# Query projections of a first attention: their evacuation moved from VectorE to ScalarE

## The reference

```
x_proj = (x @ w_in.T + b_in).reshape(b, l, 16, -1)     # 16 heads, 16 columns each for q, k, v
q, k, v = jnp.split(x_proj, 3, axis=-1)
att = jnp.einsum('blhd,bmhd->blmh', q, k) * scale      # scale = 1/sqrt(16)
att = jax.nn.softmax(att, axis=2)
opt = jnp.einsum('blmh,blhd->blhd', att, v)            # each row's own v, weighted by the sum over m
x = layernorm(x + opt @ w_out.T + b_out)
```

## Time and profile before

| | us |
|---|---|
| median of 3 runs (lowest, highest) | 3705.18 (3704.74, 3706.42) |
| the profiled execution: its time | 3707.26 |
| the profiled execution: span from first to last instruction | 3705.5 |
| busy, TensorE / VectorE / ScalarE / GpSimd | 3433.0 / 3400.8 / 2812.5 / 1788.8 |
| query evacuations on VectorE: 32 of them, busy | 23.9 |
| key evacuations on ScalarE: 32 of them, busy | 21.7 |

### The profile page before, as it was taken

How to read it: one execution, slowest core, us unless ns; L and a number is a source line. 1 busy time by engine, 2 the same in 40 slices (tenths; PEclk the granted TensorE clock), 3 DMA queues, 4 the chain that set the end, 5 groups by cost and what they waited for, 6 DMA issues and landing times. The chain is left out here.

```text
span 3705.5 us, 45135 instructions
## 1 busy us (share of the span) xinstructions
PE 3433.0 (93%) x14464; PEld 1298.0 (35%) x14464; DVE 3400.8 (92%) x5376; ACT 2812.5 (76%) x3033; POOL 1788.8 (48%) x1251
## 2 busy tenths in 40 slices
PE   8989998889999999899999999899999999899998
PEld 3334433432232324343232324343232324343333
DVE  7999999999999999889999999989999999467776
ACT  5998898778888888688888888688888887333333
POOL 4344333304444446455444446455444446758775
PEclk9999999899999999899999999899999999999999
DMA  5222222200010001200010101200000000100000
GB/s 166 80 90 93 76 83 68 83 22 18 18 29 18 29 18 41 76 16 22 18 29 18 29 18 46 70 18 21 18 29 18 29 18 18 50 1 12 12 12 12
DMA packets 117215, 142.84 MB, mean 39 GB/s; under 512 B 33394, under 2 KB 100466, under 8 KB 116978
## 3 DMA queue, kind: packets, MB, share of 16 engines
q1 hardware_dynamic: 116978, 139.95, 12.4%
HBM read 89.55 MB, written 50.33 MB: 38 GB/s over the span
## 5 line engine op out<-in xcount | busy, mean ns | idle before, releaser
L1130 ACT ACTIVATE scores<-scores,nmax 128x2048 f32<-128x2048 f32 x1024 | 2042.0, 1995 | 315.5 <-DVE scores L1321 304.4
L985 PE MATMUL ps<-stack 96*128 96x512 bf16 x4792 | 1299.9, 388 | 122.0 <-DVE scores L1321 94.9
L894 POOL TENSOR_TENSOR facc<-facc,probs 128x1024 f32<-128x1024 f32 x443 | 1049.3, 2369 | 598.1 <-ACT probs L1240 530.2
L1321 DVE TENSOR_SCALAR_CACHE_REDUCE scores<-ps,lows 128x1024 f32<-128x1024 f32 x1024 | 1278.8, 1278 | 34.3 <-PE ps L985 28.2
L1321 DVE TENSOR_SCALAR_CACHE_REDUCE scores<-ps 128x1024 f32<-128x1024 f32 x1024 | 1216.9, 1217 | 25.6 <-PE ps L985 24.4
L985 PEld LDWEIGHTS ps<-stack 96*128 96x128 bf16 x4792 | 372.7, 99 | 1168.6 <-DVE scores L1321 658.9
L1380 DVE TENSOR_REDUCE smax<-ps 128x2 f32<-128x1024 f32 x512 | 621.0, 1220 | 123.0 <-PE ps L1050 121.9
L1050 PE MATMUL ps<-fk,fq 64*128 64x512 f32 x2048 | 564.2, 632 | 60.6 <-DVE smax L1380 46.1
L1065 PE MATMUL ps<-fq,fk 64*128 64x512 f32 x2048 | 546.2, 611 | 10.6 <-DVE smax L1380 4.8
L1085 PE MATMUL ps<-probs,vals 128*64 128x512 f32 x2048 | 532.3, 615 | 4.8 <-DVE oT L1428 4.8
L1240 ACT ACTIVATE probs<-ps 128x1024 f32<-128x1024 f32 x384 | 385.4, 1012 | 88.1 <-PE ps L1068 87.7
(11 more groups left out here) (129 smaller groups left out, 2175.9 us busy)
## 6 DMA issues: line engine op xcount, KB each, us to landing
stack<-qk_levels SPq DMA_DIRECT2D x768, 64.0 KB, 2.2
qk_levels<-fk SPq DMA_DIRECT2D x64, 384.0 KB, 2.4
probs<-in_L_attn_x SPq DMA_DIRECT2D x16, 512.0 KB, 4.1
v_rows<-vals SPq DMA_DIRECT2D x16, 512.0 KB, 2.9
vrows<-v_rows SPq DMA_DIRECT2D x16, 512.0 KB, 3.3
res<-in_L_attn_x SPq DMA_DIRECT2D x16, 512.0 KB, 4.0
x_rows<-y SPq DMA_DIRECT2D x16, 512.0 KB, 2.9
res<-x_rows SPq DMA_DIRECT2D x16, 512.0 KB, 3.9
```

Of the source, the lines that this page charges most:

```text
L894: pool.tensor_tensor(total, total, probs[:, slot, :], ALU.add).then_inc(facc_ready, 1)
L985: last = pe.matmul(bank(banks[i]), stack[0:SK, hd % 2, 0, t * P:(t + 1) * P], stack[0:SK, hd % 2, 1, col:col + CH], start=True, stop=True)
L1130: act.activation(row, row, ACT.Exp, bias=nmax[:, k % LOWS:k % LOWS + 1], scale=-1.0, accum_out=esum[:, b % 2, t, hd:hd + 1]).then_inc(exp_ ...
L1321: dve.tensor_scalar(scores[:, k % ROW_SLOTS, half * TILE:(half + 1) * TILE].rearrange("p (a n) -> p a n", a=2), two_banks(banks), 1.0, fir ...
```

## The change

Query halves are evacuated by ScalarE as `Identity(scale * in + bias)`, with the scale -1/4 in the instruction. Since the bias is now added after the scaling, the two bias columns of the queries are multiplied by -1/4 once at the start (one VectorE copy of four columns becomes a multiplication of two and a copy of two). In the planner the piece `QP` moves from VectorE to ScalarE, and the planned cost of a query or key evacuation goes from 0.75 to 0.6; so the planner works out all five lists anew.

```
-        for kind, eng in (("QP", dve), ("KP", act)):
+        for kind, eng in (("QP", act), ("KP", act)):
...
-            unit(eng(*t), 0.75, [pe(*t)] + ([was("LV", *two)] if i >= 2 else []))
+            unit(eng(*t), 0.6, [pe(*t)] + ([was("LV", *two)] if i >= 2 else []))
...
+                elif kind == "QP":
+                    i = half_no[at]
+                    act.wait_ge(wT_read, 4)
+                    if i >= 2:
+                        act.wait_ge(q_split, (i - 1) * LEVEL_STEPS)
+                    act.activation(q32[:, i % 2, :], bank(banks[0]), ACT.Identity, bias=qk_bias[:, at[1]:at[1] + 1],
+                                   scale=-float(AD) ** -0.5).then_inc(q32_ready, 1)
...
-            dve.tensor_copy(qk_bias[:, :], ps[:, 3, 0:4]).then_inc(wT_read, 1)
+            dve.tensor_scalar(qk_bias[:, 0:2], ps[:, 3, 0:2], -float(AD) ** -0.5, None, ALU.mult)
+            dve.tensor_copy(qk_bias[:, 2:4], ps[:, 3, 2:4]).then_inc(wT_read, 1)
...
-                elif kind == "QP":
-                    i = half_no[at]
-                    if i >= 2:
-                        dve.wait_ge(q_split, (i - 1) * LEVEL_STEPS)
-                    dve.tensor_scalar(q32[:, i % 2, :], bank(banks[0]), qk_bias[:, at[1]:at[1] + 1], -float(AD) ** -0.5,
-                                      ALU.add, ALU.mult).then_inc(q32_ready, 1)
```

More of the change, by code:

```diff
@@ L622, in build @@
         inputs_done = max(last_user.values())
-        halves = [n[2:] for n in order["DVE"] if n[1] == "QP"]
+        halves = [n[2:] for n in order["ACT"] if n[1] == "QP"]
         half_no = {t: i for i, t in enumerate(halves)}
@@ L658, in build @@
                    ("ACT", "BC"): bc_ready, ("DVE", "C"): less_max,
-                   ("ACT", "VPh"): v_half, ("ACT", "VP"): v_copied, ("DVE", "QP"): q32_ready, ("ACT", "FQ"): fq_ready, ("ACT", "FVh"): vals_half, ("ACT", "FV"): vals_copied,
+                   ("ACT", "VPh"): v_half, ("ACT", "VP"): v_copied, ("ACT", "QP"): q32_ready, ("ACT", "FQ"): fq_ready, ("ACT", "FVh"): vals_half, ("ACT", "FV"): vals_copied,
                    ("DVE", "S"): smax_ready, ("DVE", "D"): frec_ready, ("DVE", "R"): foT_ready}
```

## The result

The change makes the kernel faster: 3686.2 us (median of 5 runs, 3680.13 to 3689.38) against 3705.57 (5 runs, 3704.74 to 3706.84). The ratio is 0.9946 with an interval of 0.9932 to 0.9961. The forecast was 3689.5, so 15.7 us gained; the medians differ by 19.4.

The account below looks back on a forecast made before the run. VectorE was taken to bound the stretch from 60 to 650 us, busy 585.45 of 590. Terms 17.2 + 3.8 - 5.2 - 0.1 = 15.7 us off 3705.2 gave 3689.5 us; range 3682 to 3699, the forecast's own 3685 to 3693.

Parts of the forecast that it names:

- The removed work: VectorE, 60 to 650 us: 26 query evacuations leave its list at a step of 0.66 us each, 17.2 us gained.
- ScalarE's instruction: ScalarE: a query evacuation takes 678 ns like the key's, its scale costs nothing; 26 x 0.59 = 15.3 us added.
- The planned alternation, +3.8: VectorE: second halves right behind their own row's first half fall from 25 to 6, 0.20 us each, 3.8 us gained.
- its lower bound: VectorE's alternation term: gain of nothing, if ScalarE is late with a row slot again and VectorE waits instead.
- ScalarE's waits, -5.2: ScalarE's evacuations that wait for TensorE's matmuls hold VectorE: 14 x 0.37 = 5.2 us lost; bounds nothing to 10.4.
- In the new list it marks 14 of 52: Count from the lists: 14 of 52 query and key evacuations on ScalarE wait for their matmuls, mostly chunks' first halves.
- 0.72 + 0.59 - 0.71 - 0.23: Per waiting evacuation: wait plus ScalarE's step, less spare per two rows and slack before VectorE is held; 0.37 us.
- The start, 0: Before the first score tile: moving six query evacuations gains 0, as key splits and loads end last; bound 4 us.
- ScalarE near its limit: ScalarE in the shortened stretch: 554.7 of some 574 us busy, 97%, just short of being the bound.
- Two signs of being wrong: PE's waiting moves onto VectorE's path; the time after 650 us changes by more than a few us.

Follow-up runs that it names:

- bias in two: Kernel before, bias column copied in two VectorE instructions, unscaled, queries still on VectorE: 3710.57 us, ratio 0.9999.
- wait filled: Kernel before, eight more 128x128 transposes on TensorE in place of its wait ahead of the first query matmuls: 3707.2 us, ratio 1.0001.
- old kernel in order: Kernel before, planner made to hand VectorE the first attention's score tiles strictly in order: 3706.55 us, ratio 0.9993.
- again: The changed kernel run once more without any edit, for a second profile: 3689.64 us, ratio 0.9944.
- start back: Changed kernel, the six query evacuations ahead of the first score tile back on VectorE: 3687.51 us, ratio 0.9935.
- wait longer: Changed kernel, two more 128x256 copies on VectorE ahead of the bias column, so TensorE waits longer: 3689.49 us, ratio 0.9951.
- old planned cost: Changed kernel, planner's cost of a query or key evacuation left at 0.75 instead of 0.6: 3691.59 us, ratio 0.9945.
- changed, in order: Changed kernel, planner made to hand VectorE the score tiles in their own order: 3690.07 us, ratio 0.9941.
- queries twice: Changed kernel, ScalarE does each of the stage's 26 query evacuations twice, first into an unread buffer: 3698.45 us, ratio 0.9964.
- the other order of tiles: Changed kernel with the planner's evacuation cost left at 0.75, giving VectorE another tile order: 3691.59 us, ratio 0.9945.

## Why the prediction was right, and where not

**The removed work: right.** 26 x 0.66 = 17.2 us was predicted; the steps add up to 17.3, and the stage is 17.8 and 19.5 us shorter in two profiles. Putting half of the queries back cost 9.7.

Stages are compared below by their parts, worked out from the steps as in the section on the result (us; profiles in the order in which the row names them, the first three and the four with the same lists on VectorE and ScalarE):

| profiles | stage | behind own row | late for ScalarE | late for TensorE |
|---|---|---|---|---|
| before; bias in two; wait filled | 601.42; 605.30; 603.92 | 5.0; 5.2; 5.1 | 0.8; 1.0; 1.0 | 1.5; 5.0; 3.7 |
| old kernel in order | 600.62 | 0 | 5.0 | 1.8 |
| changed; again; start back; wait longer | 583.60; 581.93; 581.34; 584.29 | 1.0; 1.1; 1.0; 1.0 | 2.3; 2.9; 2.3; 2.4 | 3.2; 1.1; 1.1; 3.9 |
| old planned cost | 582.47 | 4.6 | 1.0 | 0 |
| changed, in order | 587.35 | 0 | 10.3 | 0 |
| queries twice | 594.51 | 1.0 | 14.2 | 2.3 |

**ScalarE's instruction: right.** 671 ns for 678 expected, so the scale costs nothing beside the bias column, and it beats VectorE's 746. The plain copy of the values, line 1211 above, has the same shape without a bias and takes 576. The Trainium skill ("Trainium Architecture — The Big Picture", "The five engines, in one table") gives VectorE as up to about three times as fast for simple arithmetic; for this read of 512 PSUM columns the measurement is the other way round.

**The planned alternation, +3.8: the size right, a price left out.** Of the new list's 6 places the last lies behind the stage. Inside it 25 places became 5, and what they cost fell from 5.04 to 1.01 us: 4.0 gained. What the sum left out stood in its lower bound, that VectorE would wait for a late ScalarE instead. That happened in part: the lateness rose from 0.8 to 2.3 us. The other lists show the same exchange at other rates. Taking all places out of the old kernel saved 5.0 and cost 4.2. Bringing 17 back into the changed one cost 3.6 and saved 1.3. Taking out its last five saved 1.0 and cost 8. So the alternation is neither free nor a plain loss.

**ScalarE's waits, -5.2: failed twice.** This term was too large by a factor of six or more. The count: "In the new list it marks 14 of 52" became 2 waits. In the other order of tiles it was 13 of 52, and VectorE had no wait that shows there. The price: "0.72 + 0.59 - 0.71 - 0.23" subtracts 0.23 us that do not exist, as the doubled evacuations show. In the changed kernel's profile one late first half follows an evacuation that waited, by 0.33 us; in the other three profiles of these lists it is 0.25 to 0.78. What made ScalarE late instead, and what the prediction did not count, is the copy of the transposed inputs. It takes 1.00 us, and its step of 0.90 alone is more than the 0.71 to spare. Ten first halves behind it are late by 0.15 to 0.17 us. ScalarE, then VectorE, at one of them:

```profile
218.19 1.00 ACT L1136 ACTIVATE fq<-ps 128x1024 f32<-128x1024 f32 x1
219.09 1.99 ACT L1130 ACTIVATE scores<-scores,nmax 128x2048 f32<-128x2048 f32 x1
```

```profile
219.99 1.22 DVE L1329 TENSOR_SCALAR_CACHE_REDUCE scores<-ps 128x1024 f32<-128x1024 f32 x1
...
221.29 1.22 DVE L1329 TENSOR_SCALAR_CACHE_REDUCE scores<-ps 128x1024 f32<-128x1024 f32 x1
```

The kernel before has such steps of 1.30 too, five of them. No late tile of 0.41 us, the price of two evacuations in one period, shows in the changed kernel's two profiles.

**How near the sum came is in part luck.** For the stage it gave 15.8 us (17.2 + 3.8 - 5.2) and the first profile 17.8; the means of the three and the four profiles in the table are 20.8 apart. Beside the removed work the prediction had -1.4 and the profile +0.5: 4.0 from the places, -1.6 from ScalarE's lateness, -1.8 from TensorE, whose waits the prediction put at nothing and which differ by more than that between profiles of the same lists. The start's 2.07 us came on top, and 7.3 us of chance behind the stage made the profiled time lower still.

**The start, 0: mis-sized, by 2.07 us.** The prediction asked whether the splits or the loads end last. It did not look at the 1.39 us wait in the earlier trace rows, which stood there with the 3.65 us behind it. After the change:

```profile
12.34 1.98 PE L958 MATMUL ps<-fq,w_inT 128*128 128x512 f32 x4 [0.57 <-DVE qk_bias L1281]
```

A wait of 0.57 us or less goes with 1.98 us or less, one of 1.09 or more with 2.77 to 3.68, in all twelve profiles, and changing the wait alone moved the matmuls and the first tile both ways. The wait lies between two ends: TensorE's last matmuls before it, and the bias columns. Before the change, then after:

```profile
10.08 1.05 PE L931 MATMUL ps<-one,scores 1*128 1x1 f32 x8
```

```profile
10.72 1.05 PE L931 MATMUL ps<-one,scores 1*128 1x1 f32 x8
```

The wait became 0.82 us shorter mainly because TensorE was done 0.64 later. The bias columns were ready only 0.18 earlier, 12.28 for 12.46, with bias rows that arrive at 9.01 for 9.26. The changed program shows the same wait in both of its profiles. Apart from the two kernels that set the wait by hand, all five profiles with a long wait have query evacuations on VectorE, and the five with a short wait have none there. So the shorter start may belong to the change; why the two ends move by tenths of a microsecond from one program to another stays open.

**ScalarE near its limit: right.** Its idle time before exponentials was to fall to 17 us and fell to 23.1, since its evacuations waited 3.5 us where they had waited 10.1; VectorE's before first halves was to rise to 6, ended by exponentials, and rose to 2.9, of which TensorE ended 2.2. Two signs of being wrong that the prediction named came up in the first profile: more waiting for TensorE on VectorE's path, and 7.3 us less behind the stage. Both vary by as much between profiles of the same lists. 97% was expected; from 60 to 630 us it is busy 541.51 of 570 us, 95%, and the doubled evacuations, which put it over, cost 11.7 us of the stage.

## What to carry to other kernels

When two engines are both nearly full, price a move by the step on the engine that ends last, and check the taker's spare time over one period of its rhythm with the handover included: here 0.57 us into 0.71 went free, 1.14 cost 0.41. A scheduler's way around a delay is not a plain loss: before counting its removal as a gain, count the delay that comes back, here 1.6 of 4.0 us. An unchanged stage time can hide opposite parts, so add up the steps by cause. A short wait ahead of TensorE's matmuls is worth a look where they run at half their rate behind it.

## What was not expected of the hardware

TensorE's granted clock drops to the 1.2 GHz level within a kernel that keeps it 93% busy: 0.52 from 300 to 305 us, behind three waits of 0.81, 0.54 and 0.33 us, with four matmuls at 3.78 us for 1.98. The place and size differ between runs of one program (1.91 us of VectorE's time in one profile, 1.05 and 0.69 in the next). With the same lists on VectorE the part behind the stage varied by 12.6 us, more than half of the gain measured here, so a single profile could not have told the last 7 us from the edit.
